# A gated attention block with experts: the gates' copy moves behind the attention's, the last two groups are closed side by side, and GpSimd takes one addition from VectorE

## The chip, the cores and the metric

One core of one Trainium2 chip. TensorE (PE) does the matrix products, VectorE (DVE), ScalarE (ACT) and GpSimd (POOL) work on 128 partitions each, SyncE starts transfers. Each engine runs its own instructions in order; they wait for each other by semaphores. The time is the device time of one execution in microseconds (us), and a change is compared by the median of several runs.

## The reference

```python
x = x + tanh(g_xattn) * xattn(layernorm(x), ctx, ctx)            # 16 heads, 32 sequences of 128
x = x + tanh(g_ffn) * ffn(layernorm(x), ...)
# ffn: rotated causal attention, then
x1 = layer_norm(x + attn_out, ln1_w, ln1_b)
gates = softmax(x1 @ gate_w.T + gate_b)                            # 8 experts, the best two are kept
moe_out = sum(expert_outputs of the best two * their gates)
return layer_norm(x1 + moe_out, ln2_w, ln2_b)
```

x is 32 x 128 x 128 in float32. The change touches only what comes behind the second attention: its output projection, the first norm, the gates, the eight experts and the second norm.

## The kernel before

The 32 sequences are worked on in 16 groups of two. The first 333 us hold both attentions, in a schedule by slots. Behind them comes `z_steps`, a loop over steps s = 3 to 21, written once for each engine as a `body(s, c)`: the order of the instructions on an engine is that in which its body calls them, and nothing else sets it. In step s the group s is projected (`transpose_att`, `project`) and gets its first norm; group s - 1 gets its normalised rows transposed (`transpose_n`), its logits and the first four experts; group s - 2 gets its gates and experts 4 to 7; group s - 3 is summed and gets the second norm; groups s - 4 and s - 5 are scaled and stored. `in_z(c, k)` says that the group s - k exists; LAST is 15. Steps 3 to 15 are whole ones; the rest only finish.

The experts: DVE multiplies the first four by their gates and adds them up (`experts`, eight instructions on `z_acc`). ACT multiplies the last four (`gate_experts`, into `z_gated`), DVE adds them in pairs (`gated_pairs`, 128x512) and then the pairs (`gated_sum`, 128x256, into `z_gated_sum`), PE adds the result to the experts' biases in `u_bank[1]`, and DVE adds the two halves (`experts_add`, into `z_x_moe`). The very last group has no pairs: PE adds its four products itself (`last_gated_sum`).

Each norm: DVE takes statistics, moments (`z_mv`) and the negative mean (`z_minus_mean`); POOL's `factor1` and `factor2` make of them the factor and the offset, three small instructions each (`z_ve`, `z_rstd`, `z_offset`, L796, L798, L1396 and L1405); ACT applies them (`normalise1` into `z_n`, `normalise2` into `z_y`). POOL also applies the norms' weights (`x1`: `z_nw` and `z_x`; `final`: `z_yw` and `z_o`).

One bank holds both the transposed attention and the transposed rows: `transpose_n` waits until ACT has copied the attention out (`copy_att`, L1021). The logits (L912) wait for ACT's copy of the transposed rows (`copy_x1`, L1028) and, since they share a bank with the transposed gates, for the copy of the gates of the group before (`copy_gates`, L1059).

## Time and profile before

| | |
|---|---|
| median of 3 runs | 440.88 us (440.47 to 441.33) |
| the profiled execution | 440.74 us, of which its span is 438.9 us |
| PE busy | 386.6 us (88% of the span) |
| DVE busy | 369.8 us (84%) |
| POOL busy | 322.9 us (74%) |
| ACT busy | 284.2 us (65%) |
| granted TensorE clock | 0.995 over the span |

The shares are means over stages that are limited by different things. Only the last quarter of the span is touched by the change, and it is read by itself: the timeline of each engine there gives the start and the length of every instruction, and in brackets the idle time before it with what ended it.

### The profile page before, as it was taken

Reading aid. Unit: us, or ns where it says so; the run is one execution under the profiler, and the core shown is the slowest. Engines: PE = TensorE matmul, PEld = TensorE weight load, DVE = VectorE, ACT = ScalarE, POOL = GpSimd, SP = SyncE. Lnnn points to the kernel's source line nnn. Section 1 sums busy time; section 2 is a strip of 40 time slices with the busy share of each in tenths; the row PEclk is TensorE's granted clock in tenths of the full one; section 3 lists DMA queues with packets and bytes.
Section 4 is the critical chain, followed back from the end, with each engine's and each line's share of the span. In section 5 each row is a group of like instructions: output and inputs, shape, how many; then the busy total and the mean of one; then the engine's idle time right before and its main releaser. Section 6 shows DMA issues by size and latency. Waiting matters only on the chain.

```text
span 438.9 us, 17690 instructions
## 1 busy us (share of the span) xinstructions
PE 386.6 (88%) x6538; PEld 231.7 (53%) x6538; DVE 369.8 (84%) x1219; ACT 284.2 (65%) x728; POOL 322.9 (74%) x712
## 2 busy tenths in 40 slices
PE   0368888888888899999999999999999999999994
PEld 0134544444444556666666666666665555555541
DVE  6587999999997877888877877878858999999987
ACT  1126777767776666666666666666665687787782
POOL 4456767767779988888888888874322688888885
PEclk9999999999999999999999999999999999999997
DMA  6756686665553333343334444333000000000001
GB/s 164 194 155 159 160 208 176 163 172 148 132 158 101 98 100 101 103 110 101 102 102 120 117 114 116 102 105 96 12 4 2 1 24 15 24 26 13 25 24 50
DMA packets 88037, 42.76 MB, mean 97 GB/s; under 512 B 16000, under 2 KB 87824, under 8 KB 87952
## 3 DMA queue, kind: packets, MB, share of 16 engines
q1 hardware_dynamic: 80864, 39.59, 33.9%
q10 hardware_dynamic: 7088, 2.04, 2.0%
q8 instruction: 53, 0.87, 0.9%
q14 instruction: 32, 0.26, 0.2%
HBM read 5.69 MB, written 2.10 MB: 18 GB/s over the span
## 4 chain that ended last, share of the span: by engine, by line
PE 48%; DVE 6%; issue 2%; ACT 2%; POOL 1%; POOLq 0%; DVEq 0%
PE u_bank L499 9%; PE s_bank L926 6%; PE st_bank L926 6%; PE s_bank L421 5%; PE s_bank L434 4%; DVE r L697 2%; PE u_bank L945 2%; PE t_bank L413 2%; PE u_bank L912 2%; PE t_bank L407 2%; PE m_bank L889 2%; PE u_bank L514 1%; PE u_bank L950 1%; PE t_bank L900 1%; ACT part L577 1%
## 5 line engine op out<-in xcount | busy, mean ns | idle before, releaser
L716 DVE TENSOR_REDUCE nm<-s_bank 128x4 f32<-128x512 f32 x256 | 171.5, 682 | 36.2 <-PE s_bank L434 33.9
L599 ACT ACTIVATE pt<-st_bank 128x512 f32<-128x512 f32 x250 | 147.4, 602 | 73.7 <-PE st_bank L434 51.2
L434 PE MATMUL s_bank<-qk 64*64 64x128 bf16 (+1 forms) x1584 | 103.6, 220 | 12.2 <-DVE nm L716 6.9
L499 PE MATMUL u_bank<-pt,vaug 128*32 128x128 f32 x2048 | 108.3, 286 | 1.7
L434 PE MATMUL st_bank<-qk 64*64 64x128 bf16 (+1 forms) x1540 | 98.2, 218 | 0.0
L434 PEld LDWEIGHTS s_bank<-qk 64*64 64x64 bf16 (+1 forms) x1584 | 73.9, 104 | 36.2 <-issue 18.9
L434 PEld LDWEIGHTS st_bank<-qk 64*64 64x64 bf16 (+1 forms) x1540 | 69.2, 103 | 0.0
L499 PEld LDWEIGHTS u_bank<-pt,vaug 128*32 128x32 f32 x2048 | 41.2, 108 | 27.6 <-issue 5.2
L421 PE MATMUL s_bank<-mqk,idb 64*64 64x256 bf16 x256 | 38.3, 292 | 0.5 <-ACT pt L599 0.4
L327 POOL TENSOR_TENSOR part<-r,part 128x512 bf16<-128x512 f32 x32 | 37.1, 1159 | 1.4
L421 PE MATMUL st_bank<-mkq,idb 64*64 64x256 bf16 x244 | 35.7, 293 | 0.0
L338 POOL TENSOR_SCALAR mst<-nm 128x16 bf16<-128x16 f32 x64 | 13.2, 207 | 27.7 <-DVE nm L716 27.7
L606 ACT ACTIVATE mts<-m_bank 128x128 bf16<-128x128 bf16 x63 | 17.5, 278 | 24.8 <-PE m_bank L509 24.8
L514 PE MATMUL u_bank<-idf,us 128*128 128x128 f32 x128 | 28.0, 301 | 5.2 <-ACT us L615 4.9
L796 POOL TENSOR_SCALAR z_ve<-z_mv 128x2 f32<-128x2 f32 x32 | 13.0, 405 | 26.5 <-DVE z_minus_mean L1162 22.6
L1068 ACT ACTIVATE z_gated<-st_bank,z_gates 128x128 f32<-128x128 f32 x120 | 31.5, 343 | 0.0
L926 PE MATMUL s_bank<-ewt,z_x_t 128*128 128x512 f32 x64 | 31.4, 613 | 0.0
L926 PE MATMUL st_bank<-ewt,z_x_t 128*128 128x512 f32 x64 | 30.2, 594 | 0.0
L322 POOL TENSOR_SCALAR part<-r 128x512 bf16<-128x512 f32 x32 | 19.9, 620 | 10.8 <-DVE r L692 6.3
L421 PEld LDWEIGHTS s_bank<-mqk,idb 64*64 64x64 bf16 x256 | 14.4, 103 | 24.3 <-issue 14.3
L1231 DVE SCALAR_TENSOR_TENSOR z_acc<-s_bank,z_gates,z_acc 128x128 f32<-128x128 f32 x96 | 26.1, 341 | 0.0
L280 POOL TENSOR_TENSOR rstd<-ve,mhalf 128x2 f32<-128x2 f32 x32 | 22.8, 713 | 2.7
(138 smaller groups left out, 828.2 us busy)
## 6 DMA issues: line engine op xcount, KB each, us to landing
qk<-part SPq DMA_DIRECT2D x221, 128.0 KB, 2.8
x_all<-x SPq DMA_DIRECT2D x16, 128.0 KB, 2.6
qk<-qrow SPq DMA_DIRECT2D x32, 64.0 KB, 2.2
c_all<-ctx_in SPq DMA_DIRECT2D x14, 128.0 KB, 2.6
out<-z_o SPq DMA_DIRECT2D x14, 128.0 KB, 1.8
qk<-mts ACTq DMA_DIRECT2D x34, 32.0 KB, 2.6
qk<-mts SPq DMA_DIRECT2D x30, 32.0 KB, 2.0
ewt<-exp_t SPq DMA_DIRECT2D x1, 512.0 KB
```

The source lines that it names most:

```text
L280: pool.tensor_tensor(rstd[u % 2][:, :], ve[u % 2][:, :], mhalf[:, :], ALU.pow).then_inc(rstd_s, 1)
L322: pool.tensor_scalar(part[u % 2][:, 1:2 * PARTS:PARTS, :], r32[:, :].rearrange("c (o t) -> c o t", o=2), 1.0, 0.0, ALU.mult, ALU.add).then ...
L327: pool.tensor_tensor(part[u % 2][:, 2:2 * PARTS:PARTS, :], r32[:, :].rearrange("c (o t) -> c o t", o=2), part[u % 2][:, 1:2 * PARTS:PARTS, ...
L421: pe.matmul(to, idb[rows, rows], mask[rows, rows].unsqueeze(1).broadcast_to([64, HEADS, 64]), start=True, stop=False, skip_group_check=True)
L434: ins = pe.matmul(to[outs, :], fixed[:, outs], moving, start=not masked, stop=True, skip_group_check=masked)
L499: ins = pe.matmul(u_bank[b][32 * j:32 * j + 32, r * P:(r + 1) * P], v, pt[m % 4][:, j, :], start=half == 0, stop=half == 1, skip_group_che ...
L514: ins = pe.transpose(u_bank[q % 2][:, W + r * P:W + (r + 1) * P], us[q % 2][:, r * P:(r + 1) * P], idf[:, :])
L599: act.activation(pt[m % 4][:, :, :].rearrange("k j q -> k (j q)"), transposed_bank(m)[:, :], ACT.Exp).then_inc(ex, 1)
L716: dve.tensor_reduce(nm[q % 2][:, first:first + HEADS], s_bank[n % 2][:, :].rearrange("q (j k) -> q j k", j=HEADS), AX_X, ALU.max, negate=T ...
L926: ins = pe.matmul(e_bank[b][k][:, :], zx1t[i][:, b * P:(b + 1) * P], ewt[:, k * 512:(k + 1) * 512], start=True, stop=True)
L1068: ins = act.activation(zyg[:, b, e, :], e_bank[b][1][:, e * P:(e + 1) * P], ACT.Copy, scale=zg[i][:, b, HALF + e:HALF + e + 1])
L1231: dve.scalar_tensor_tensor(out=zacc[i][e % 2][:, b, :], in0=e_bank[b][0][:, e * P:(e + 1) * P], scalar=zg[i][:, b, e:e + 1], in1=zacc[i][( ...
```

## The change

1. ACT copies the gates (`copy_gates`) right behind `copy_att` and ahead of `copy_x1`, except for the last group.
2. `gated_sum`, the addition of the two pairs, goes from DVE to POOL, between `factor1` and `factor2`, for the groups 0 to 13. Group 14's stays on DVE.
3. DVE takes the first norm's moments ahead of the second norm's statistics, and the pairs come ahead of the second norm's `experts_minus_mean`. `factor1` starts when the moments are there; only its third instruction waits for the negative mean. `factor2` likewise.
4. The last two groups: their sums, statistics and moments are taken side by side in the last step, `factor2(14)` moves there, and PE transposes the gates of group 14 ahead of the rows of group 15. On ACT `normalise2` of group 13 goes behind the last experts.

```diff
--- before.py
+++ after.py
@@ -842,8 +842,9 @@
         def rstd_steps(g):
             return 2 * g if g <= 2 else 3 * g - 2
 
-        def all_steps(g):
-            return (g + 1) * ALL - (1 if g == LAST else 0)
+        def moments_done(g):
+            both = (LAST - 1) * ALL + G + G * G
+            return (g + 1) * ALL - 1 if g < LAST - 1 else both + (g - LAST + 2) * G
 
         def in_z(c, lag):
             return 0 <= c - lag < GROUPS
@@ -966,10 +967,11 @@
                 if in_z(c, 0):
                     transpose_att(s, c)
                 if s - 1 == LAST:
+                    gates_t(s - 2, c - 2)
                     transpose_n(s - 1, c - 1)
                 if in_z(c, 3) and s - 3 < LAST:
                     sum_of_biases(s - 3, c - 3)
-                if in_z(c, 2):
+                if in_z(c, 2) and s - 1 != LAST:
                     gates_t(s - 2, c - 2)
                 if in_z(c, 1) and s - 1 < LAST:
                     transpose_n(s - 1, c - 1)
@@ -1083,14 +1085,10 @@
             def body(s, c):
                 if in_z(c, 0):
                     copy_att(s, c)
+                if in_z(c, 2) and s - 2 < LAST:
+                    copy_gates(s - 2, c - 2)
                 if in_z(c, 1):
                     copy_x1(s - 1, c - 1)
-                if in_z(c, 4) and s - 2 == LAST:
-                    normalise2(s - 4, c - 4)
-                if s - 2 == LAST:
-                    gate_last_experts(s - 2, c - 2)
-                if in_z(c, 2):
-                    copy_gates(s - 2, c - 2)
                 if in_z(c, 2) and s - 2 < LAST:
                     gate_experts(s - 2, c - 2, 0)
                     if s - 1 == LAST:
@@ -1098,7 +1096,10 @@
                     gate_experts(s - 2, c - 2, 1)
                     if s - 1 < LAST:
                         gates_exp(s - 1, c - 1)
-                if in_z(c, 4) and s - 2 < LAST:
+                if s - 2 == LAST:
+                    gate_last_experts(s - 2, c - 2)
+                    copy_gates(s - 2, c - 2)
+                if in_z(c, 4) and s - 4 < LAST - 1:
                     normalise2(s - 4, c - 4)
                 if in_z(c, 0):
                     normalise1(s, c)
@@ -1192,7 +1193,7 @@
                 add_gate_bias(g, gc)
                 logit_maxima(g, gc)
 
-            def gating(g, gc, second_level=None):
+            def gating(g, gc):
 
 
                 i = gc % 2
@@ -1208,8 +1209,6 @@
                 dve.wait_ge(z_gate, k + 6)
                 for b in range(G):
                     dve.match_replace(zq[:, b, :], z8[:, b, :], zp[:, b, :], 0.0).then_inc(z_gate, 1)
-                if second_level is not None:
-                    gated_sum(*second_level)
                 dve.wait_ge(z_gate, k + 9)
                 dve.tensor_tensor(zt[:, :, :], zp[:, :, :], zq[:, :, :], ALU.subtract).then_inc(z_gate, 1)
                 dve.wait_ge(z_gate, k + 10)
@@ -1260,20 +1259,19 @@
             def experts_stats(g, gc):
                 k = g * ALL
                 y = zsum[g % 2]
-                dve.wait_ge(z_all, k + 1)
+                dve.wait_ge(z_all, k + 1 if g < LAST - 1 else (LAST - 1) * ALL + G)
                 for b in range(G):
                     dve.bn_stats(zst2[g % 2][:, b, :], y[:, b, :]).then_inc(z_all, 1)
 
             def experts_moments(g, gc):
                 k = g * ALL
-                dve.wait_ge(z_all, k + 1 + G)
+                dve.wait_ge(z_all, k + 1 + G if g < LAST - 1 else (LAST - 1) * ALL + G + G * G)
                 for b in range(G):
                     dve.bn_aggr(zmv2[g % 2][:, b, :], zst2[g % 2][:, b, :]).then_inc(z_all, 1)
 
             def experts_minus_mean(g, gc):
-                if g < LAST:
-                    dve.wait_ge(z_all, (g + 1) * ALL - 1)
-                    dve.tensor_scalar(zmn2[g % 2][:, :], zmv2[g % 2][:, :, 0], -1.0, 0.0, ALU.mult, ALU.add).then_inc(z_all, 1)
+                dve.wait_ge(z_all, (g + 1) * ALL - 1)
+                dve.tensor_scalar(zmn2[g % 2][:, :], zmv2[g % 2][:, :, 0], -1.0, 0.0, ALU.mult, ALU.add).then_inc(z_all, 1)
 
 
             def all_experts(g, gc):
@@ -1284,7 +1282,7 @@
 
             def weigh(g):
                 i = g % 2
-                dve.wait_ge(z_all, all_steps(g))
+                dve.wait_ge(z_all, moments_done(g))
                 for b in range(G):
                     dve.scalar_tensor_tensor(out=zyc[i][:, b, :], in0=zsum[i][:, b, :], scalar=zmv2[i][:, b, 0:1],
                                              in1=l2w[:, :], op0=ALU.subtract, op1=ALU.mult).then_inc(z_yw, 1)
@@ -1302,7 +1300,9 @@
                 if in_z(c, 2) and s - 2 < LAST:
                     if in_z(c, 3):
                         gated_pairs(s - 3, c - 3)
-                    gating(s - 2, c - 2, (s - 3, c - 3) if in_z(c, 3) else None)
+                    if in_z(c, 4):
+                        experts_minus_mean(s - 4, c - 4)
+                    gating(s - 2, c - 2)
                 if s - 2 == LAST:
                     gating(s - 2, c - 2)
                     gated_pairs(s - 3, c - 3)
@@ -1312,24 +1312,25 @@
                 if in_z(c, 0):
                     attention_add(s, c)
                     experts_add(s - 3, c - 3)
+                    attention_stats(s, c)
                     add_gate_bias(s - 1, c - 1)
-                    attention_stats(s, c)
+                    attention_moments(s, c)
                     logit_maxima(s - 1, c - 1)
                     experts_stats(s - 3, c - 3)
-                    attention_moments(s, c)
+                    attention_minus_mean(s, c)
                     experts_moments(s - 3, c - 3)
-                    attention_minus_mean(s, c)
-                    experts_minus_mean(s - 3, c - 3)
                 else:
                     if s - 1 == LAST:
                         shift_logits(s - 1, c - 1)
-                    if in_z(c, 3):
+                    if s - 3 == LAST - 2:
                         all_experts(s - 3, c - 3)
-                    if s - 3 == LAST - 1:
+                    if s - 3 == LAST:
+                        for step in (experts_add, experts_stats, experts_moments):
+                            step(LAST - 1, c - 4)
+                            step(LAST, c - 3)
                         weigh(LAST - 1)
-                    if s - 3 == LAST:
+                        weigh(LAST)
                         close(LAST - 1)
-                        weigh(LAST)
                         close(LAST)
 
             def early(n):
@@ -1372,6 +1373,12 @@
                 pool.tensor_tensor(zx1[i][:, :, :], zw[:, :, :], l1b[:, :].unsqueeze(1).broadcast_to([P, G, P]),
                                    ALU.add).then_inc(z_x1, 1)
 
+            def gated_sum(g, gc):
+                pool.wait_ge(z_yp, g + 1)
+                if gc >= 1:
+                    pool.wait_ge(z_yb, g)
+                pool.tensor_tensor(zyq[:, :, :], zyp[:, :, 0, :], zyp[:, :, 1, :], ALU.add).then_inc(z_yq, 1)
+
             def final(g, gc):
                 i = gc % 2
                 pool.wait_ge(z_y2s, (g + 1) * G)
@@ -1387,27 +1394,30 @@
 
             def factor1(g, gc):
                 i = gc % 2
-                pool.wait_ge(z_h, (g + 1) * H1)
+                pool.wait_ge(z_h, (g + 1) * H1 - 1)
                 if gc >= 2:
                     pool.wait_ge(z_n, (g - 1) * G)
                 rstd_of(pool, zmv[i][:, :, 1], zve[i][:, :], zrs[i][:, :], z_rs, rstd_steps(g))
                 if g >= 2:
                     pool.wait_ge(z_rs, rstd_steps(g) + 2)
+                    pool.wait_ge(z_h, (g + 1) * H1)
                     pool.tensor_tensor(znb[i][:, :], zmn[i][:, :], zrs[i][:, :], ALU.mult).then_inc(z_rs, 1)
 
             def factor2(g, gc):
                 i = g % 2
-                pool.wait_ge(z_all, all_steps(g))
+                pool.wait_ge(z_all, moments_done(g))
                 k = g * 3 if g < LAST else (LAST - 1) * 3 + 2
                 rstd_of(pool, zmv2[i][:, :, 1], zve2[i][:, :], zrs2[i][:, :], z_rs2, k)
                 if g < LAST - 1:
                     pool.wait_ge(z_rs2, k + 2)
+                    pool.wait_ge(z_all, (g + 1) * ALL)
                     pool.tensor_tensor(znb2[i][:, :], zmn2[i][:, :], zrs2[i][:, :], ALU.mult).then_inc(z_rs2, 1)
 
             def body(s, c):
                 if in_z(c, 1):
                     x1(s - 1, c - 1)
                 if s - 3 == LAST:
+                    factor2(s - 4, c - 4)
                     factor2(s - 3, c - 3)
                 if in_z(c, 5) and s - 5 < LAST - 2:
                     final(s - 5, c - 5)
@@ -1415,7 +1425,8 @@
                     final(s - 4, c - 4)
                 if in_z(c, 0):
                     factor1(s, c)
-                if in_z(c, 3) and s - 3 < LAST:
+                    gated_sum(s - 2, c - 2)
+                if in_z(c, 3) and s - 3 < LAST - 1:
                     factor2(s - 3, c - 3)
 
             def early(n):
@@ -1441,6 +1452,7 @@
 
             def steps():
                 factor1(2, 2)
+                gated_sum(0, 0)
                 z_steps(body)
 
             return early, steps
```

DVE in a whole step of before (`z_h` is the sum behind the first norm, `z_x_moe` that behind the second; `z_mv_1` and `z_minus_mean_1` belong to the second norm, as does any name there with a number):

```order
L1144 TENSOR_TENSOR z_h<-m_bank,xn_all 128x256
L1257 TENSOR_TENSOR z_x_moe<-u_bank,z_acc 128x256
L1183 TENSOR_TENSOR z_logit<-u_bank,gbb 128x16
L1151 BN_STATS z_stats<-z_h 128x6 x2
L1189 TENSOR_REDUCE z_max<-z_logit 128x2
L1265 BN_STATS z_stats_1<-z_x_moe 128x6 x2
L1157 BN_AGGR z_mv<-z_stats 128x2 x2
L1271 BN_AGGR z_mv_1<-z_stats_1 128x2 x2
L1162 TENSOR_SCALAR z_minus_mean<-z_mv 128x2
L1276 TENSOR_SCALAR z_minus_mean_1<-z_mv_1 128x2
L1240 TENSOR_TENSOR z_gated_pairs<-z_gated 128x512
```

and the same place now:

```order
L1145 TENSOR_TENSOR z_h<-m_bank,xn_all 128x256
L1256 TENSOR_TENSOR z_x_moe<-u_bank,z_acc 128x256
L1152 BN_STATS z_stats<-z_h 128x6 x2
L1184 TENSOR_TENSOR z_logit<-u_bank,gbb 128x16
L1158 BN_AGGR z_mv<-z_stats 128x2 x2
L1190 TENSOR_REDUCE z_max<-z_logit 128x2
L1264 BN_STATS z_stats_1<-z_x_moe 128x6 x2
L1163 TENSOR_SCALAR z_minus_mean<-z_mv 128x2
L1270 BN_AGGR z_mv_1<-z_stats_1 128x2 x2
L1239 TENSOR_TENSOR z_gated_pairs<-z_gated 128x512
L1274 TENSOR_SCALAR z_minus_mean_1<-z_mv_1 128x2
L1203 MAX z_sorted<-z_exps 128x8 x2
```

The first norm's moments (`z_mv`) now come ahead of the maxima and of the second statistics, and the pairs ahead of the second negative mean; the addition into `z_gated_sum`, which stood further down ahead of `z_top`, is gone.

POOL in a whole step of before:

```order
L1367 TENSOR_TENSOR z_nw<-z_n,l1w 128x256
L1372 TENSOR_TENSOR z_x<-z_nw,l1b 128x256
L1380 TENSOR_TENSOR z_yw<-z_y,l2w 128x256
L1386 TENSOR_TENSOR z_o<-z_yw,x_all 128x256
L796 TENSOR_SCALAR z_ve<-z_mv 128x2
L798 TENSOR_TENSOR z_rstd<-z_ve,mhalf 128x2
L1396 TENSOR_TENSOR z_offset<-z_minus_mean,z_rstd 128x2
L796 TENSOR_SCALAR z_ve_1<-z_mv_1 128x2
L798 TENSOR_TENSOR z_rstd_1<-z_ve_1,mhalf 128x2
L1405 TENSOR_TENSOR z_offset_1<-z_minus_mean_1,z_rstd_1 128x2
```

and now:

```order
L1368 TENSOR_TENSOR z_nw<-z_n,l1w 128x256
L1373 TENSOR_TENSOR z_x<-z_nw,l1b 128x256
L1387 TENSOR_TENSOR z_yw<-z_y,l2w 128x256
L1393 TENSOR_TENSOR z_o<-z_yw,x_all 128x256
L796 TENSOR_SCALAR z_ve<-z_mv 128x2
L798 TENSOR_TENSOR z_rstd<-z_ve,mhalf 128x2
L1404 TENSOR_TENSOR z_offset<-z_minus_mean,z_rstd 128x2
L1380 TENSOR_TENSOR z_gated_sum<-z_gated_pairs 128x256
L796 TENSOR_SCALAR z_ve_1<-z_mv_1 128x2
L798 TENSOR_TENSOR z_rstd_1<-z_ve_1,mhalf 128x2
L1414 TENSOR_TENSOR z_offset_1<-z_minus_mean_1,z_rstd_1 128x2
```

The addition stands between the two norms' factors.

DVE at the end of before, from the last product of group 15 on:

```order
L1231 SCALAR_TENSOR_TENSOR z_acc<-s_bank,z_gates,z_acc 128x128 x6
L1257 TENSOR_TENSOR z_x_moe<-u_bank,z_acc 128x256
L1265 BN_STATS z_stats_0<-z_x_moe 128x6 x2
L1271 BN_AGGR z_mv_0<-z_stats_0 128x2 x2
L1276 TENSOR_SCALAR z_minus_mean_0<-z_mv_0 128x2
L1289 SCALAR_TENSOR_TENSOR z_yc<-z_x_moe,z_mv_0,l2w 128x128 x2
L1257 TENSOR_TENSOR z_x_moe<-t_bank,z_acc 128x256
L1265 BN_STATS z_stats_1<-z_x_moe 128x6 x2
L1271 BN_AGGR z_mv_1<-z_stats_1 128x2 x2
L1298 SCALAR_TENSOR_TENSOR z_o<-z_yc,z_rstd_0,x_all 128x128 x2
L1289 SCALAR_TENSOR_TENSOR z_yc<-z_x_moe,z_mv_1,l2w 128x128 x2
L1298 SCALAR_TENSOR_TENSOR z_o<-z_yc,z_rstd_1,x_all 128x128 x2
```

and now:

```order
L1256 TENSOR_TENSOR z_x_moe<-u_bank,z_acc 128x256
L1256 TENSOR_TENSOR z_x_moe<-t_bank,z_acc 128x256
L1264 BN_STATS z_stats_0<-z_x_moe 128x6 x2
L1264 BN_STATS z_stats_1<-z_x_moe 128x6 x2
L1270 BN_AGGR z_mv_0<-z_stats_0 128x2 x2
L1270 BN_AGGR z_mv_1<-z_stats_1 128x2 x2
L1287 SCALAR_TENSOR_TENSOR z_yc<-z_x_moe,z_mv_0,l2w 128x128 x2
L1287 SCALAR_TENSOR_TENSOR z_yc<-z_x_moe,z_mv_1,l2w 128x128 x2
L1296 SCALAR_TENSOR_TENSOR z_o<-z_yc,z_rstd_0,x_all 128x128 x2
L1296 SCALAR_TENSOR_TENSOR z_o<-z_yc,z_rstd_1,x_all 128x128 x2
```

Both sums come first and both closing pairs last, and the negative mean of group 14 is gone.

## Rows read from the trace of the kernel before

**Rows 1.** Timeline: PE: start us, length us, engine, line, operation, count.

```profile
416.26 0.28 PE L935 MATMUL u_bank<-idf,z_gates 128*16 128x128 f32 x1
416.65 0.41 PE L900 MATMUL t_bank<-idf,z_n 128*128 128x128 f32 x2
...
417.95 0.58 PE L912 MATMUL u_bank<-gwt,z_x_t 128*128 128x8 f32 x4
...
423.87 0.28 PE L935 MATMUL u_bank<-idf,z_gates 128*16 128x128 f32 x1
423.98 0.60 PE L950 MATMUL u_bank<-z_gated_sum,idf 128*128 128x256 f32 x2
```

**Rows 2.** Timeline: DVE, the period from 411.38 us, same columns.

```profile
411.38 0.42 DVE L1144 TENSOR_TENSOR z_h<-m_bank,xn_all 128x256 f32<-128x256 f32 x1 [0.25 <-PE m_bank L889]
...
412.53 0.15 DVE L1189 TENSOR_REDUCE z_max<-z_logit 128x2 f32<-128x16 f32 x1
...
412.99 0.23 DVE L1157 BATCH_NORM_AGGREGATE z_mv<-z_stats 128x2 f32<-128x6 f32 x2
...
413.47 0.69 DVE L1240 TENSOR_TENSOR z_gated_pairs<-z_gated 128x512 f32<-128x512 f32 x1
...
414.76 0.42 DVE L1247 TENSOR_TENSOR z_gated_sum<-z_gated_pairs 128x256 f32<-128x256 f32 x1
415.09 0.17 DVE L1214 TENSOR_TENSOR z_top<-z_exps,z_others 128x16 f32<-128x16 f32 x1
...
417.97 0.42 DVE L1144 TENSOR_TENSOR z_h<-m_bank,xn_all 128x256 f32<-128x256 f32 x1 [0.25 <-PE m_bank L889]
```

**Rows 3.** Timeline: POOL, the same period.

```profile
413.51 0.70 POOL L796 TENSOR_SCALAR z_ve<-z_mv 128x2 f32<-128x2 f32 x1 [0.47 <-DVE z_minus_mean L1162]
414.30 0.70 POOL L798 TENSOR_TENSOR z_rstd<-z_ve,mhalf 128x2 f32<-128x2 f32 x1
415.08 0.25 POOL L1396 TENSOR_TENSOR z_offset<-z_minus_mean,z_rstd 128x2 f32<-128x2 f32 x1
415.41 0.19 POOL L796 TENSOR_SCALAR z_ve<-z_mv 128x2 f32<-128x2 f32 x1
...
416.45 0.20 POOL L1405 TENSOR_TENSOR z_offset<-z_minus_mean,z_rstd 128x2 f32<-128x2 f32 x1
416.61 0.73 POOL L1367 TENSOR_TENSOR z_nw<-z_n,l1w 128x256 f32<-128x256 f32 x1
417.41 0.73 POOL L1372 TENSOR_TENSOR z_x<-z_nw,l1b 128x256 f32<-128x256 f32 x1
418.09 0.73 POOL L1380 TENSOR_TENSOR z_yw<-z_y,l2w 128x256 f32<-128x256 f32 x1
```

**Rows 4.** Timeline: ACT, the same period.

```profile
415.36 0.88 ACT L1045 ACTIVATE z_n<-z_h,z_offset,z_rstd 128x128 f32<-128x128 f32 x2 [0.98 <-POOL z_offset L1396]
...
417.09 0.56 ACT L1028 ACTIVATE z_x_t<-t_bank,l1bc,l1wc 128x256 f32<-128x256 f32 x1 [0.59 <-PE t_bank L900]
417.56 0.25 ACT L1059 ACTIVATE z_gates_t<-u_bank 16x128 f32<-16x128 f32 x1
```

**Rows 5.** Timeline: POOL in the attention, a large instruction and a small one.

```profile
157.17 1.16 POOL L327 TENSOR_TENSOR part<-r,part 128x512 bf16<-128x512 f32 x1
158.42 0.20 POOL L277 TENSOR_SCALAR ve<-mv 128x2 f32<-128x2 f32 x1
```

**Rows 6.** Timeline: POOL and DVE at the same time in step 17.

```profile
428.68 0.72 POOL L1380 TENSOR_TENSOR z_yw<-z_y,l2w 128x256 f32<-128x256 f32 x1
428.69 0.98 DVE L1247 TENSOR_TENSOR z_gated_sum<-z_gated_pairs 128x256 f32<-128x256 f32 x1
```

**Rows 7.** Timeline: the end: timelines of DVE and, last row, POOL.

```profile
429.60 0.60 DVE L1231 SCALAR_TENSOR_TENSOR z_acc<-s_bank,z_gates,z_x 128x128 f32<-128x128 f32 x2
...
433.65 0.41 DVE L1257 TENSOR_TENSOR z_x_moe<-t_bank,z_acc 128x256 f32<-128x256 f32 x1
...
434.96 0.20 POOL L796 TENSOR_SCALAR z_ve<-z_mv 128x2 f32<-128x2 f32 x1 [0.65 <-DVE z_mv L1271]
```

## The prediction

> **What bounds the kernel now.** The chain that ended last comes first: from 333 us on it lies on PE almost alone, which reads as if PE were the limit. The timeline of each engine over one period behind 400 us corrects that. From one `z_h` to the next are 417.97 - 411.38 = 6.59 us [rows 2], and each of the steps 3 to 15 repeats it. In it PE stands still twice. Between the transposed gates and the transposed rows lie 0.39 us, where the same instruction gives way after 0.11 in the next step, in another place [rows 1]: 0.28 us of waiting, for ACT, which copies the attention only after its normalisation. And the logits at 417.95 come after the copy of the gates, which ends at 417.56 + 0.25 = 417.81, while the rows themselves were copied at 417.09 + 0.56 = 417.65 [rows 4]: 0.16 us, at most 0.18. PE's own work is 6.59 - 0.28 - 0.18 = 6.13 us a step. So the period is a loop: `z_h`, statistics, moments and negative mean on DVE, three instructions on POOL, normalisation on ACT (idle 0.98 us for POOL's offset [rows 4]), copy, transposes, projection, `z_h`.
>
> Inside the loop one row is odd. POOL's first `z_ve` takes 0.70 us, the second, on equal shapes, 0.19 [rows 3]. It starts at 413.51, just behind the start of the pairs on DVE, 413.47 to 414.16 [rows 2]: it is held up by 0.51 us and ends 0.05 behind them. The reverse is in [rows 6]: a DVE addition that alone takes 0.42 [rows 2] takes 0.98 because a POOL addition began 0.01 us before it; it goes on about 0.14 ahead of POOL's end (428.68 + 0.72 - 0.14 = 429.26, and 429.26 + 0.42 = 429.68). So these two kinds shut each other out, and the loser's own time starts 0.14 ahead of the winner's end.
>
> **Part 1, gates copied earlier.** Nothing is added. The logits come 0.16 to 0.18 earlier on PE; the copy itself (0.16 us of ACT's queue) goes ahead of `z_x_t`, where ACT is idle for 0.59 [rows 4]. Taken alone it cuts the loop by nothing, as the logits aren't on it; it lowers what PE needs.
>
> **Part 2 and 3, the loop.** DVE loses the addition, 415.09 - 414.76 = 0.33 us, but the wait that it covered (`z_others` to `z_top`) shows: about 0.11 comes back. The new order costs about 0.06 in waits on the statistics. DVE needs about 6.1 us a step. `z_ve` may start after the moments. Before, it started 413.51 - 411.38 = 2.13 behind `z_h`. The maxima and the second statistics, 412.99 - 412.53 = 0.46 [rows 2], no longer stand ahead of the moments, nor do the second moments and the negative mean (0.20); the wait for the statistics takes 0.03 to 0.05 of it back: 1.50. From the unhindered start of `z_ve` to the start of `z_n`: 0.28 + (415.36 - 414.30 = 1.06) = 1.34 [rows 3, 4]. From there to `z_h`: 417.97 - 415.36 = 2.61 [rows 2, 4]. The loop shrinks to 1.50 + 1.34 + 2.61 = 5.45 us and stops being the limit.
>
> **What is late next** is POOL. Its queue, start to start, from [rows 3]: `z_ve` 0.27; `z_rstd` 415.08 - 414.30 = 0.78; `z_offset` 416.61 - 416.45 = 0.16; the new addition 0.81; `z_ve` 0.27 and `z_rstd` 0.77 (together 416.45 - 415.41 = 1.04); `z_offset` 0.16; `z_nw` 417.41 - 416.61 = 0.80; `z_x` 0.68; `z_yw` 0.81 as `z_nw`, since the next one needs its result; `z_o` 0.81. The sum is 6.32 us. No row shows the addition on POOL. I take 0.73 us, the time of the four other additions and products of this shape, and 0.08 until a small `z_ve` follows, as in 415.08 + 0.25 = 415.33 to 415.41 [rows 3] and 157.17 + 1.16 = 158.33 to 158.42 behind a large one [rows 5]. The lower bound lets the next instruction start 0.04 ahead of the end, as `z_x` to `z_yw` does: 0.69 in place of 0.81 at two places, sum 6.08. The upper bound is the longest hold-up seen, 0.51, on top. A gain is excluded: the work is added.
>
> **The pairs meet POOL.** POOL's queue is 6.32 long and the loop 5.45, so `z_ve` comes to its turn 0.87 us after its moments are there, 1.50 + 0.87 = 2.37 behind `z_h`, and `z_o` stands ahead of it from 1.56 to 2.29. On DVE the pairs come to their turn 413.47 - 411.38 = 2.09 behind `z_h`, less the negative mean that went behind them, plus waits: about 2.06 [rows 2]. That is inside `z_o`. DVE waits until 2.29 - 0.14 = 2.15, runs the 0.69 us to 2.84, and `z_ve` goes on at 2.84 - 0.14 = 2.70 in place of 2.37. That is 0.33 us for POOL, the limit: 6.65 us a step. The hold-up lengthens the queue and the loop alike, so it does not move out of its own way.
>
> The Trainium skill (SBUF — State Buffer, "SBUF: two separate sides") says the port pair that DVE and GpSimd share is an exclusive lock, taken by a DVE operation with two SBUF inputs against a GpSimd one that reads SBUF, and that the loser is blocked until about 115 ns behind DVE's end. The trace agrees on the lock [rows 3, 6] and not on the length: `z_ve` would have ended at 414.16 + 0.12 + 0.19 = 414.47 and ended at 414.21. By the page's figure a step would take 6.90 us by estimate and the kernel 443 us.
>
> **The sum.** Steps 3 and 4 have no `z_yw` and `z_o` on POOL and no collision: PE's 6.13, taken as 6.16 with the loop's joints, saves 2 x 0.43 = 0.86. While POOL falls behind, the two steps after them meet the pairs at other instructions; laid forward by hand they take about 6.47 and save 2 x 0.12 = 0.24. The eight periods to step 15 cost 8 x 0.06 = 0.5 more. So the last `z_h` comes 0.6 us earlier.
>
> **The end (part 4).** Before, from the start of the last products at 429.60 [rows 7] to the end of the last `z_o` are 7.00 us, with the last sum at 433.65, 4.05 behind. Now that sum waits only for PE's last additions, which ACT feeds 0.8 us earlier: it comes 3.14 behind. But both groups' statistics and POOL's factors now follow one another. Sum 0.33, statistics 0.39 twice, moments 0.13 and 0.22 and 0.09: POOL starts 4.6 behind, held up by 0.17 by DVE's products; `z_ve` 0.27 and `z_rstd` 0.78 for group 14, again 0.17, then the same for 15; last, 0.61 for the closing pair: 7.6. In before the last `z_ve` started 434.96 - 429.60 = 5.36 behind [rows 7], now 5.9. That is 0.6 lost. Ahead of it, the earlier gates of group 14 and ACT's shorter queue save 0.2, and the 0.56 that DVE lost in [rows 6] is a tie of 0.01 us that may fall either way: 0 to 0.7. The end costs between -0.3 and +0.4. Total: -0.9 to -0.2; I take -0.45. On the profiled execution's 440.74 us (the median of the runs is 0.14 above it) that is 440.3 us. A measurement can tell about 0.2% here, 0.9 us: 440.0 to 441.76 is no change.
>
> **Rivals.** (A) The forecast, POOL bound with the pairs in its way, 440.3 us: chance 0.50, of which 0.1 falls below 440.0. (B) POOL bound but the pairs find a gap: 6.32 a step. For it: in [rows 6] the order was decided by 0.01 us. Against: the arithmetic puts the pairs 0.2 us inside `z_o`. Ten steps x 0.27 + 0.86 = 3.6 saved: 437.1 us, chance 0.22. (C) Slower: the hold-up is dearer than 0.33. The pairs come so late in `z_o`, or `z_ve` loses to them so early, that the whole 0.51 of [rows 3] is paid, or the offset is held up too (0.05 of its 0.25 us, [rows 3]). It decides from 6.67 us a step on, where the gain of the first steps is gone. At 6.80 it is 10 x 0.21 - 0.86 = +1.2: 442.0 us; with both, 6.32 + 0.51 + 0.05 = 6.88, it is 442.8. Chance 0.20. By the figure of the Trainium skill's page above it would end in this rival as well. (D) The addition finds room: POOL's queue at its lower bound of 6.08 lies below PE's 6.13, and 12 steps x 0.43 go: 435.6 us, chance 0.08. That the copy of the gates doesn't free the logits, because the transposed gates come late, changes nothing while POOL is the limit.
>
> **The numbers.** Faster 0.1 + 0.22 + 0.08 = 0.40; slower 0.18, most of C; within 0.2% 0.42. The range leaves out D and the upper part of C: 436.8 to 442.2; A alone has 439.8 to 441.2.
>
> **What would show it.** ACT's gates' copy ahead of `z_x_t` and no gap over 0.05 ahead of the logits: part 1. POOL without idle from step 6 on, `z_o`, `z_ve` and the pairs within 0.3 us, `z_ve` about 0.5 long and the pairs over 0.8: A. The same with `z_ve` 0.19: B. Periods of 6.16 in steps 3 and 4, then 6.65. At the end `z_ve` of both groups 1.2 us apart. Wrong is the forecast if POOL still idles ahead of `z_ve`.

## The result, and the profile after

The changed kernel takes 443.19 us (median of 6 runs, 442.65 to 444.04), the kernel before 440.91 us beside it (440.47 to 441.33). The ratio is 1.0053 with a 95% interval of 1.0040 to 1.0066: slower by 2.3 us, more than a measurement can miss, and outside the range of the prediction. The profiled execution has a time of 443.27 us and a span of 441.4 us, 2.5 more than before.

| | before | after |
|---|---|---|
| `z_h` of step 3 to step 4, us | 6.59 | 6.08 |
| steady period, us | 6.59 | 6.86 |
| last `z_h` starts, us | 417.97 | 419.21 |
| from there to the end of the last `z_o` on DVE, us | 18.62 | 19.80 |

The table shows both halves of the loss. The first `z_h` of the steps already stands 0.2 us late; steps 2 to 4 give back 0.05 + 0.51 + 0.52; then come 6.48, 6.63 and eight periods of 6.86, 0.27 longer than before: the last `z_h` is 1.24 us late. The end is 1.18 us longer.

The busy times of the page (first row before, second after): POOL took over DVE's additions and more.

```profile
PE 386.6 (88%) x6538; PEld 231.7 (53%) x6538; DVE 369.8 (84%) x1219; ACT 284.2 (65%) x728; POOL 322.9 (74%) x712
```

```profile
PE 384.0 (87%) x6538; PEld 231.9 (53%) x6538; DVE 370.2 (84%) x1204; ACT 285.6 (65%) x728; POOL 330.6 (75%) x726
```

DVE runs 15 instructions fewer and is busy 0.4 us longer: something there now takes longer than its work. One steady period, timeline of DVE after (start us, length us, engine, line, operation); it answers to [rows 2]:

```profile
398.63 0.42 DVE L1145 TENSOR_TENSOR z_h<-m_bank,xn_all 128x256 f32<-128x256 f32 x1 [0.34 <-PE m_bank L890]
...
399.81 0.25 DVE L1158 BATCH_NORM_AGGREGATE z_mv<-z_stats 128x2 f32<-128x6 f32 x2
...
400.03 0.48 DVE L1264 BATCH_NORM_STATS2 z_stats<-z_x_moe 128x6 f32<-128x128 f32 x2
400.42 0.58 DVE L1163 TENSOR_SCALAR z_minus_mean<-z_mv 128x2 f32<-128x2 f32 x1
400.92 0.23 DVE L1270 BATCH_NORM_AGGREGATE z_mv<-z_stats 128x2 f32<-128x6 f32 x2
401.08 0.65 DVE L1239 TENSOR_TENSOR z_gated_pairs<-z_gated 128x512 f32<-128x512 f32 x1
401.65 0.15 DVE L1274 TENSOR_SCALAR z_minus_mean<-z_mv 128x2 f32<-128x2 f32 x1
```

And POOL in the same period, where [rows 3] had five large instructions and a wait:

```profile
400.26 0.72 POOL L1393 TENSOR_TENSOR z_o<-z_yw,x_all 128x256 f32<-128x256 f32 x1
401.06 0.71 POOL L796 TENSOR_SCALAR z_ve<-z_mv 128x2 f32<-128x2 f32 x1
401.86 0.70 POOL L798 TENSOR_TENSOR z_rstd<-z_ve,mhalf 128x2 f32<-128x2 f32 x1
402.64 0.20 POOL L1404 TENSOR_TENSOR z_offset<-z_minus_mean,z_rstd 128x2 f32<-128x2 f32 x1
402.80 0.73 POOL L1380 TENSOR_TENSOR z_gated_sum<-z_gated_pairs 128x256 f32<-128x256 f32 x1
403.61 0.19 POOL L796 TENSOR_SCALAR z_ve<-z_mv 128x2 f32<-128x2 f32 x1
```

Read them side by side. POOL has no idle time any more: it is the limit. Its `z_o` starts at 400.26, `z_minus_mean` on DVE at 400.42. The same operation on the same shape takes 0.15 us at 401.65 and 0.58 here; it ends at 401.00, which is `z_o`'s end less 0.14 (400.84) plus its own 0.15. So `z_o` holds it up by 0.43. Behind it everything on DVE is later, and the pairs start at 401.08, 0.02 us after `z_ve` on POOL (401.06). It is `z_ve` that loses all the same, though its record starts first: its 0.19 become 0.71, and it ends 0.04 behind the pairs. This chain of two hold-ups repeats in each steady period; its price for POOL, the limit, is 0.52 us: 6.33 us of queue + 0.52 = 6.85.

### The profile page after: what moved, and what is told of

It is laid out like the page before. It is cut to its first block, busy times and chain, and to the rows that moved or that the text cites. A ratio compares the mean times of both kernels' runs of the same rounds, so it can differ in the third digit from the quotient of the medians.

```text
span 441.4 us, 17717 instructions
## 1 busy us (share of the span) xinstructions
PE 384.0 (87%) x6538; PEld 231.9 (53%) x6538; DVE 370.2 (84%) x1204; ACT 285.6 (65%) x728; POOL 330.6 (75%) x726
## 4 chain that ended last, share of the span: by engine, by line
PE 33%; DVE 14%; POOL 4%; issue 3%; ACT 3%; POOLq 0%; DVEq 0%; ACTq 0%
PE u_bank L499 9%; PE s_bank L421 5%; PE s_bank L434 4%; DVE r L697 2%; PE t_bank L413 2%; DVE z_acc L1230 2%; PE t_bank L407 2%; POOL z_ve L796 2%; POOL z_rstd L798 2%; DVE z_stats L1264 1%; PE u_bank L514 1%; DVE z_x_moe L1256 1%; ACT part L577 1%; DVE z_stats L1152 1%; PE m_bank L890 1%
## 5 line engine op out<-in xcount | busy, mean ns | idle before, releaser
L1070 ACT ACTIVATE z_gated<-st_bank,z_gates 128x128 f32<-128x128 f32 x120 | 32.5, 383 | 0.0
L796 POOL TENSOR_SCALAR z_ve<-z_mv 128x2 f32<-128x2 f32 x32 | 11.7, 367 | 19.9 <-DVE z_mv L1158 16.5
L798 POOL TENSOR_TENSOR z_rstd<-z_ve,mhalf 128x2 f32<-128x2 f32 x32 | 22.9, 716 | 2.7
```

The lines of the kernel that those rows point to most:

```text
L796: pool.tensor_scalar(v_eps, v_in, 1.0, EPS, ALU.mult, ALU.add).then_inc(semaphore, 1)
L798: pool.tensor_tensor(r_out, v_eps, mhalf[:, :], ALU.pow).then_inc(semaphore, 1)
L1070: ins = act.activation(zyg[:, b, e, :], e_bank[b][1][:, e * P:(e + 1) * P], ACT.Copy, scale=zg[i][:, b, HALF + e:HALF + e + 1])
```

## The experiments

The table puts all kernels beside each other; "after the last `z_h`" is the time to the end of the last `z_o`, and both it and the period are of the profiled execution alone. The kernels before that ran beside them had medians of 440.72 us (the first four), 440.92 (the next four) and 440.91 (the last).

| kernel | median us | ratio to before, 95% | period | after the last `z_h` |
|---|---|---|---|---|
| after | 443.19 | 1.0040 to 1.0066 | 6.86 | 19.80 |
| before, gates copied early | 440.53 | 0.9979 to 1.0006 | 6.59 | 18.36 |
| after, sum back on DVE | 437.06 | 0.9901 to 0.9933 | 6.29 | 18.49 |
| after, means by a reduction | 441.08 | 0.9998 to 1.0024 | 6.65 | 20.59 |
| after, end as before | 442.11 | 1.0027 to 1.0063 | 6.85 | 18.94 |
| after, sum on DVE, end as before | 436.69 | 0.9884 to 0.9914 | 6.29 | 17.85 |
| the same, means by a reduction | 436.49 | 0.9879 to 0.9908 | 6.29 | 17.86 |
| after, POOL's factor and sum first | 441.20 | 0.9998 to 1.0027 | 6.62 | 18.81 |
| before, only the sum on POOL | 443.06 | 1.0027 to 1.0061 | 6.79 | 19.26 |
| before, only DVE's new order | 436.22 | 0.9878 to 0.9911 | 6.29 | 17.31 |

**The gates' copy alone.** The kernel before with part 1, and PE transposing the gates first in the last step:

```diff
                 if in_z(c, 0):
                     copy_att(s, c)
+                if in_z(c, 2) and s - 2 < LAST:
+                    copy_gates(s - 2, c - 2)
                 if in_z(c, 1):
                     copy_x1(s - 1, c - 1)
...
-                if in_z(c, 2):
+                if s - 2 == LAST:
                     copy_gates(s - 2, c - 2)
```

> The kernel before with part 1 alone: ACT copies the gates right behind the attention, and PE transposes the gates of group 14 ahead of the rows of group 15. Theory (the period is the loop over POOL's factor, the logits are not on it): the period stays 6.59 us, the logits come 0.16 us earlier and wait for nothing; 440.9 us, between 440.5 and 441.4. Rival (the logits are on the path): 12 x 0.16 = 1.9 us less, 439.0 us.

Measured 440.53 us, period 6.59: no change, as forecast. ACT copies the gates ahead of `z_x_t`, the logits start 0.20 us ahead of `z_h` (404.41 and 404.61) where they started 0.02 ahead, and the period does not move: the logits are not on the loop.

**The sum back on DVE.** The changed kernel without part 2:

```diff
                     dve.match_replace(zq[:, b, :], z8[:, b, :], zp[:, b, :], 0.0).then_inc(z_gate, 1)
+                if second_level is not None:
+                    gated_sum(*second_level)
...
                     factor1(s, c)
-                    gated_sum(s - 2, c - 2)
```

> The changed kernel with the second level of the gated sum back on DVE, all else kept. Theory (POOL's queue, 6.33 us with the addition and 6.86 with what DVE does to it, is the limit): without the addition POOL's queue is 5.5 us, it idles ahead of z_ve, z_ve takes 0.19 and the negative mean 0.15; the period falls to about 6.3 us and the kernel to 438.5 us, between 437.5 and 439.5. Rival (the moments ahead of the second statistics, or the side by side end, made it slower): 442 us or more.

Measured 437.06 us: 6.1 us below the changed kernel, and 0.8% below the kernel before. POOL in a period:

```profile
395.85 0.73 POOL L1395 TENSOR_TENSOR z_o<-z_yw,x_all 128x256 f32<-128x256 f32 x1
397.30 0.19 POOL L796 TENSOR_SCALAR z_ve<-z_mv 128x2 f32<-128x2 f32 x1 [0.72 <-DVE z_mv L1158]
```

POOL waits 0.72 us for the moments again, `z_o` is long over when DVE takes the mean, and `z_ve` takes its 0.19. Now DVE has no idle time and its queue of 6.29 us is the period (one period, from 382.92 us on, is 6.59: DVE starts its pairs late with no wait that the profile names; the other runs with 6.29 have such a period in about the same place, and its cause is open). The period is the expected one; the total is 1.4 us better than expected and just outside the stated 437.5 to 439.5. The whole loss comes with the sum's move, and hardly any of it is work: of the 6.86 - 6.29 = 0.57 us a period 0.52 are the hold-up, and POOL's queue alone (6.33) is 0.04 longer than this period. Another 1.3 us lie behind the last `z_h`.

**The two means as a reduction.** In the changed kernel the negative mean of both norms is taken by an instruction of another kind, on the same values:

```diff
-dve.tensor_scalar(zmn[i][:, :], zmv[i][:, :, 0], -1.0, 0.0, ALU.mult, ALU.add).then_inc(z_h, 1)
+dve.tensor_reduce(zmn[i][:, :], zmv[i][:, :, 0:1], AX_X, ALU.max, negate=True).then_inc(z_h, 1)
```

> The changed kernel, but both negative means are taken by a TENSOR_REDUCE over one element with its sign turned (same values) in place of a TENSOR_SCALAR. Theory (the TENSOR_SCALAR, though it has one input, is held up by POOL's z_o for 0.43 us and so brings the pairs exactly onto z_ve, which then waits 0.52): the reduction takes 0.15 us, the pairs come 0.4 us earlier and wait inside z_o, z_ve takes about 0.5 in place of 0.72, the period falls from 6.86 to about 6.65 us and the kernel to 441.1 us. Rival (any small DVE instruction is held up there, or the moments themselves come late): the period stays 6.86 and the time 443.2 us.

Measured 441.08 us. This is the run that isolates the step that failed. DVE, then POOL:

```profile
398.87 0.13 DVE L1163 TENSOR_REDUCE z_minus_mean<-z_mv 128x2 f32<-128x2 f32 x1
398.98 0.25 DVE L1270 BATCH_NORM_AGGREGATE z_mv<-z_stats 128x2 f32<-128x6 f32 x2
399.15 0.83 DVE L1239 TENSOR_TENSOR z_gated_pairs<-z_gated 128x512 f32<-128x512 f32 x1
```

```profile
398.70 0.73 POOL L1393 TENSOR_TENSOR z_o<-z_yw,x_all 128x256 f32<-128x256 f32 x1
399.51 0.51 POOL L796 TENSOR_SCALAR z_ve<-z_mv 128x2 f32<-128x2 f32 x1
```

The reduction starts inside `z_o` (398.70 to 399.43) and takes 0.13 us: it is not held up. The pairs come 2.08 us behind `z_h` (397.07), still inside `z_o`, wait, run to 399.98, and hold `z_ve` for 0.51 - 0.19 = 0.32 in place of 0.52. That is the prediction's picture, number by number: pairs at 2.06, hold-up 0.33, period 6.65; and the two periods behind step 5 are 6.48 each, where the prediction had 6.47 twice. Five of its ten executions lie between 440.79 and 440.95, half a microsecond above the forecast's 440.3, with an end that is longer than forecast; four lie at 441.9 to 442.5, and the last section shows what one of them has more.

**The end as before**, in the changed kernel: the pair before last is summed and weighed first, the last pair behind it.

```diff
-                    if s - 3 == LAST - 2:
+                    if s - 3 < LAST - 1:
                         all_experts(s - 3, c - 3)
-                    if s - 3 == LAST:
+                    if s - 3 in (LAST - 1, LAST):
                         for step in (experts_add, experts_stats, experts_moments):
...
-                    factor2(s - 4, c - 4)
                     factor2(s - 3, c - 3)
```

> The changed kernel with the end of DVE and POOL as before: group 14 is summed, and its factors taken, in its own step, and group 15's behind it. Theory (the side by side end costs about 0.4 us, since both groups' factors follow one another on POOL behind the last moments): 442.8 us. Rival (the end is long because POOL arrives late, whatever the order): 443.2 us or more, and if side by side is a gain, up to 443.9 us.

Measured 442.11 us, and 18.94 us behind the last `z_h` against 19.80: the order of the end costs 0.86 us, twice what was expected, and the median lies below the expected 442.8. The end of the changed kernel on DVE, answering to [rows 7], and its POOL:

```profile
431.10 0.59 DVE L1230 SCALAR_TENSOR_TENSOR z_acc<-s_bank,z_gates,z_x 128x128 f32<-128x128 f32 x2
...
434.32 0.42 DVE L1256 TENSOR_TENSOR z_x_moe<-t_bank,z_acc 128x256 f32<-128x256 f32 x1 [0.74 <-PE t_bank L962]
434.78 0.87 DVE L1264 BATCH_NORM_STATS2 z_stats<-z_x_moe 128x6 f32<-128x128 f32 x4
435.69 0.38 DVE L1270 BATCH_NORM_AGGREGATE z_mv<-z_stats 128x2 f32<-128x6 f32 x4
...
438.40 0.61 DVE L1296 SCALAR_TENSOR_TENSOR z_o<-z_yc,z_rstd,x_all 128x128 f32<-128x128 f32 x2 [0.60 <-POOL z_rstd L798]
```

```profile
436.02 0.35 POOL L796 TENSOR_SCALAR z_ve<-z_mv 128x2 f32<-128x2 f32 x1 [1.11 <-DVE z_mv L1270]
436.46 0.70 POOL L798 TENSOR_TENSOR z_rstd<-z_ve,mhalf 128x2 f32<-128x2 f32 x1
437.24 0.35 POOL L796 TENSOR_SCALAR z_ve<-z_mv 128x2 f32<-128x2 f32 x1
437.68 0.69 POOL L798 TENSOR_TENSOR z_rstd<-z_ve,mhalf 128x2 f32<-128x2 f32 x1
```

DVE idles 0.74 us for PE with the earlier group's statistics undone; then both groups' statistics and both factors on POOL stand one behind the other, and DVE idles 0.60 more for the last of them.

**Sum on DVE and the old end** (the second and the fourth run's edits together):

> The changed kernel with the second level of the gated sum back on VectorE inside the gating, and with the end of VectorE and GpSimd ordered as in the kernel before (the pair before last weighed first, the last pair behind it). The run with only the sum put back took 437.06 us with a period of 6.29 us and 18.49 us from the last attention sum to the end; the run with only the old end was 0.85 us shorter behind its last attention sum than the changed kernel (18.94 against 19.79). Theory (the loop's time is set by the meetings of GpSimd's long additions with small VectorE operations, the end costs on its own by its order): period again 6.29, last attention sum at about 414.7, end 17.7 to 18.2 behind it, 436.3 us (435.9 to 436.9). Rival (in the run with the sum put back the order of the end is hidden, because VectorE arrives there earlier by the same amount as everything else and waits for the same products): 437.06 again, within 0.3.

Measured 436.69 us, 17.85 us behind the last `z_h` against 18.49: the order of the end counts here too. Between the medians it is 0.4 us, hardly more than a few runs can tell.

**The same with reductions** (the third run's edit on top):

> The same kernel as the one with the sum on VectorE and the old end, and both negative means taken as a tensor_reduce (max, negated) over one element instead of a tensor_scalar. There no GpSimd addition is in flight when the means are taken (in the run with the sum on VectorE the tensor_scalar took 0.15 us), so theory: nothing to win, 0.01 us a step at most, same period 6.29 and same time within 0.2 us. Rival (a tensor_scalar also takes something from GpSimd, or the reduction shifts the order of arrivals so that another operation is held up): period off by more than 0.05, time off by 0.5 us or more.

Measured 436.49 us, period 6.29. As expected, the kind of instruction is worth nothing where no addition of POOL is in flight: the gain of the third run was the hold-up, not a quicker instruction.

**POOL's factor and sum first.** The same instructions in another order:

```diff
-                if in_z(c, 5) and s - 5 < LAST - 2:
-                    final(s - 5, c - 5)
...
                 if in_z(c, 0):
                     factor1(s, c)
                     gated_sum(s - 2, c - 2)
+                if in_z(c, 5) and s - 5 < LAST - 2:
+                    final(s - 5, c - 5)
```

> The changed kernel with GpSimd's queue in another order: the factor of the attention norm and the second level of the sum ahead of the final weigh-and-add of the pair five steps back (z_yw, z_o), instead of behind them; all instructions are the same, so GpSimd's queue is still 6.33 us of work. Theory (the lost time is two hold-ups that hang on where z_o stands: z_o holds up VectorE's negative mean, which pushes the pairs onto GpSimd's z_ve): with z_o behind, neither mean nor z_ve is held up (0.15 and 0.19 us), at most a gate operation meets one of GpSimd's long additions (0.4 us on VectorE, off the path of GpSimd), so the period is 6.33 to 6.5, last attention sum near 415.8 to 416.5, total 438.5 to 439.5 us, faster than before by 1.2 to 2.2 us. Rival (the cost of the addition is GpSimd's port contention in general, whatever the order): period 6.8 to 6.9, 443 us.

Measured 441.20 us, period 6.62, last `z_h` at 417.66: theory and rival both missed their numbers. The price of the sum does hang on POOL's order, so it is not the same whatever the order; but the period is above the expected 6.33 to 6.5, and the time above the expected 438.5 to 439.5. Neither the mean (0.15) nor `z_ve` (0.19) is held up any more. In their place:

```profile
399.87 0.66 DVE L1239 TENSOR_TENSOR z_gated_pairs<-z_gated 128x512 f32<-128x512 f32 x1
...
401.32 0.73 DVE L1213 TENSOR_TENSOR z_top<-z_exps,z_others 128x16 f32<-128x16 f32 x1
```

```profile
399.59 0.71 POOL L798 TENSOR_TENSOR z_rstd<-z_ve,mhalf 128x2 f32<-128x2 f32 x1
400.38 0.21 POOL L1404 TENSOR_TENSOR z_offset<-z_minus_mean,z_rstd 128x2 f32<-128x2 f32 x1
400.61 0.73 POOL L1380 TENSOR_TENSOR z_gated_sum<-z_gated_pairs 128x256 f32<-128x256 f32 x1
401.29 0.72 POOL L1387 TENSOR_TENSOR z_yw<-z_y,l2w 128x256 f32<-128x256 f32 x1
```

`z_top`, 0.17 us of work, starts 0.03 us behind `z_yw` and takes 0.73. The gates and the experts come 0.56 later. DVE is never idle in this period, and its queue is 6.29 - 0.33 (the sum gone) + 0.11 (the wait that it covered, the prediction's figure) + 0.56 = 6.63. The expectation had allowed a gate operation to lose 0.4 us, off GpSimd's path; it lost 0.56, and DVE, never idle here, sets the period. Moving the large additions moves the hold-up to another small operation; it does not go.

**Only the sum on POOL**, in the kernel before:

```diff
-                    gating(s - 2, c - 2, (s - 3, c - 3) if in_z(c, 3) else None)
+                    gating(s - 2, c - 2)
...
                     factor1(s, c)
+                    gated_sum(s - 2, c - 2)
```

> The kernel before with only one part of the change: the second level of the gated sum on GpSimd between its two factors; VectorE keeps its old order (gate bias and maxima ahead of the moments, the two negative means behind), the gates are copied late, and the end is the old one. Theory (GpSimd's queue is then the bound, and its z_ve waits for moments that come late): mean and z_ve are both held up, period 6.8 to 6.9, last attention sum at about 420.5, total 443 to 444 us, slower than the changed kernel by 0 to 1 us. Rival (the early moments of the change are what makes the meetings of z_o with the mean, and the old order has none): period 6.3 to 6.5, 438 to 440 us.

Measured 443.06 us, at the lower end of the theory's range, and 0.1 below the changed kernel, not above it. Period 6.79, just under the expected 6.8, the mean held up by 0.32 and `z_ve` by 0.43:

```profile
401.07 0.47 DVE L1162 TENSOR_SCALAR z_minus_mean<-z_mv 128x2 f32<-128x2 f32 x1
```

```profile
400.79 0.72 POOL L1392 TENSOR_TENSOR z_o<-z_yw,x_all 128x256 f32<-128x256 f32 x1
401.63 0.62 POOL L796 TENSOR_SCALAR z_ve<-z_mv 128x2 f32<-128x2 f32 x1
```

The nearest relative is the changed kernel with the old end (442.11 us, period 6.85), which has DVE's new order and the early gates besides. In the steady steps the new order is then worth nothing: what it gives is taken back by the meetings. Only the first steps gain (6.08 where this kernel has 6.52). The end of this run is not quite comparable: its profile has PE at a granted clock of 0.52 from 427.00 to 430.00, and from the last products to the end it takes 7.43 us where before has 7.00; all four executions have the same mean clock, 0.992. The sum's price depends on what stands beside it: 2.1 us here, in DVE's old order, and 6.1 us in the new one.

**Only DVE's new order**, in the kernel before. The moments go ahead, the second negative mean goes behind the pairs, the sum stays. The end keeps its old order, without the negative mean of group 14:

```diff
                     attention_add(s, c)
                     experts_add(s - 3, c - 3)
+                    attention_stats(s, c)
                     add_gate_bias(s - 1, c - 1)
-                    attention_stats(s, c)
+                    attention_moments(s, c)
                     logit_maxima(s - 1, c - 1)
                     experts_stats(s - 3, c - 3)
-                    attention_moments(s, c)
                     attention_minus_mean(s, c)
...
-                pool.wait_ge(z_h, (g + 1) * H1)
+                pool.wait_ge(z_h, (g + 1) * H1 - 1)
```

> The kernel before with only VectorE's reordering: attention moments ahead of the logit maxima, the expert moments last, the experts' negative mean moved behind the pairs, and GpSimd's factors released by the moments instead of by the means. The sum stays on VectorE, the gates are copied late, the end is the old one; it is the run of the sum on VectorE with the old end (436.69 us, period 6.29) without the early copy of the gates. Theory (the reordering is what wins: VectorE's pairs no longer meet z_ve, and the early copy of the gates is not on the loop here either): period 6.29, 436.5 to 437.0 us. Rival (with the loop at 6.29 us and TensorE's own need at 6.13 us, the earlier gates copy now carries part of it): period 6.35 to 6.45, 437.5 to 439 us.

Measured 436.22 us, period 6.29, ratio 0.9895 (0.9878 to 0.9911): the fastest of all. DVE has no idle time in the period. One part of the change holds the whole gain:

```profile
395.76 0.41 DVE L1144 TENSOR_TENSOR z_h<-m_bank,xn_all 128x256 f32<-128x256 f32 x1
...
397.83 0.66 DVE L1240 TENSOR_TENSOR z_gated_pairs<-z_gated 128x512 f32<-128x512 f32 x1
398.40 0.16 DVE L1275 TENSOR_SCALAR z_minus_mean<-z_mv 128x2 f32<-128x2 f32 x1
```

```profile
397.27 0.19 POOL L796 TENSOR_SCALAR z_ve<-z_mv 128x2 f32<-128x2 f32 x1 [0.72 <-DVE z_mv L1157]
397.55 0.71 POOL L798 TENSOR_TENSOR z_rstd<-z_ve,mhalf 128x2 f32<-128x2 f32 x1
```

`z_ve` is over (397.46) before the pairs start (397.83).

Stacked by medians from before: DVE's order -4.7 us; the gates' early copy with its order in the last steps +0.5 (436.22 to 436.69, with overlapping intervals; it is not shown to cost); the side-by-side end +0.4; the sum on POOL +6.1: together +2.3.

## Why the prediction was wrong

**What held.** The limit before was a loop and not PE; without it the loop falls below the queues (6.29 in four runs). Part 1 alone gives nothing. The addition costs 0.73 us and 0.08 on POOL, the queue is 6.33 (6.32), POOL has no idle time. `z_o` stands 1.63 to 2.35 behind `z_h` (1.56 to 2.29). The steps 3 and 4 gained 0.51 and 0.52 (0.43), those behind them came to 6.48 and 6.63 (6.47 twice). The lock's release 0.14 us ahead of the winner's end gives the measured end of every hold-up here to within 0.03.

**The step that failed** is the one that brings the pairs to their turn on DVE about 2.06 behind `z_h`. It carried `z_minus_mean` at its 0.15 us through `z_o`, because I had read the lock as one of DVE operations with two SBUF inputs. The mean has one. It is held up all the same, by 0.43: the pairs come at 401.08 - 398.63 = 2.45, not in `z_o` but just behind `z_ve`, which pays 0.52 and not 0.33. 6.86 instead of 6.65, over eight periods 1.7 us. The forecast worked with the rows at hand, which show a large operation against a large one and `z_ve` against the pairs; no row of before shows the mean beside a POOL addition, and that unknown should have been bounded from 0 to 0.5 us, as the text did for the addition. The run with reductions confirms the rest of the step: with the mean free, the pairs come at 2.08 and the period is 6.65.

The Trainium skill has the half of the rule that I left out. In the section that I cited (SBUF — State Buffer, "SBUF: two separate sides"), the lock is also taken by an operation in a mode that uses both of DVE's read ports; and (VectorE: DVE Perf Modes, "The perf-mode tier table") `tensor_scalar` on fp32 in SBUF has such a mode, `tensor_reduce` has only the plain one. The traces fit both: inside POOL's `z_o` the one takes 0.58 us and the other 0.13, down to two elements a partition. They don't show which mode an instruction runs in, so that this is the reason is not shown; that the kind of instruction decides is.

**The rival.** This was (C): the whole 0.51 is paid, 6.86 a step where it said 6.80 to 6.88, 443.27 us where it said 442.0 to 442.8. Its condition, pairs so late that `z_ve` pays in full, was given a small chance; the mean made it the rule. The estimate of 6.90 us a step and 443 us that the prediction worked out from the Trainium skill's figure comes near by luck: it had the pairs inside `z_o` and a release behind the winner's end, and neither is what the trace shows.

**The end** was mis-sized: 7.91 us (439.01 - 431.10) from the last products, not 7.6, where before has 7.00. The sum came at 3.22 (3.14), `z_ve` at 4.92 behind (4.6). Part of that is adding up: the prediction's own terms give 4.69 and then 7.74. The rest is that the terms for the sum and the four statistics had back-to-back spacing, where each now waits for the one ahead of it (0.46 for 0.33, and 0.91 for 0.78). The tie of [rows 6] was lost again (`z_gated_sum` 0.98 us). Forecast -0.3 to +0.4, measured +0.9 for the seven-us stretch; 0.26 more lie between the last `z_h` and those products, where the experts' mean, held up by `z_o` on POOL from 427.71 on, takes 0.41 us and not 0.15:

```profile
428.06 0.41 DVE L1274 TENSOR_SCALAR z_minus_mean<-z_mv 128x2 f32<-128x2 f32 x1
```

**Sum.** Forecast -0.6 for the last `z_h`, measured +1.24: 1.7 of it the hold-up, 0.2 a later start, less 0.1 for better first steps. Forecast +0.15 for the end, measured +1.18. The chance that I gave to slower, 0.18, rested on (C) alone being an accident.

## What to carry to other kernels

Before work goes from DVE to GpSimd, write down for one period which large GpSimd operations will be in flight and every DVE operation that starts inside them, small ones with one SBUF input too; each may pay up to the rest of the GpSimd operation, and what it pushes back can then hold up GpSimd in turn. Where no row shows the pair in question, bound it from nothing to the whole. Test the parts of a change one by one: here one reordering was worth 4.7 us, and the offload that came with it cost 6.1, though in the kernel before it alone cost 2.1. Let the last groups follow each other rather than march side by side when one wait stands ahead of both.

## What the runs showed of the hardware

**Small instructions count in full.** A `tensor_scalar` over two elements a partition lost 0.43 us to an addition on GpSimd, a `tensor_reduce` on the same values nothing. Nor did the statistics lose: the two of `z_h` start at 399.30, inside GpSimd's `z_x` (398.77, 0.73 us), and take 0.47 us, as long as two take in the kernel before at 432.11 with GpSimd idle (0.48).

**Not every `tensor_scalar` loses.** The attention of the kernel before has one with two per-partition scalars that starts inside GpSimd's own, and takes the 0.34 us that it also takes at 161.30, where GpSimd's had ended. Whether DVE's instruction or GpSimd's makes the difference no run here tells:

```profile
201.64 0.84 POOL L284 TENSOR_SCALAR xn_all<-x_all,mv,rstd 128x128 f32<-128x128 f32 x1
```

```profile
202.00 0.34 DVE L684 TENSOR_SCALAR xn_all<-x_all,mv,rstd 128x128 f32<-128x128 f32 x1
```

**The length of a GpSimd instruction is not what blocks.** `z_rstd` takes 0.70 us on two elements, as long as an addition over 256. In the run with the factor first, DVE's pairs start at 399.87, inside it (399.59 to 400.30), and take their 0.66 us, unhindered. Yet it is held up itself when the pairs start first, here in the changed kernel by 0.45 us (DVE, then POOL):

```profile
353.28 0.66 DVE L1239 TENSOR_TENSOR z_gated_pairs<-z_gated 128x512 f32<-128x512 f32 x1
```

```profile
353.36 1.15 POOL L798 TENSOR_TENSOR z_rstd<-z_ve,mhalf 128x2 f32<-128x2 f32 x1
```

**The clock falls in some executions.** In the profiled one of the kernel with reductions, the granted clock by windows (length, PE busy, PEclk, DMA share, GB/s):

```profile
421.00:422.00 1.00, 0.28 (x2) 1.00 0.00 0
422.00:424.00 2.00, 2.00 (x11) 1.00 0.03 8
424.00:427.00 3.00, 3.00 (x5) 0.51 0.01 3
427.00:428.00 1.00, 1.00 (x3) 0.77 0.40 121
```

From 424.0 on PE has 1.2 instead of 2.4 GHz for about 3.4 us. It had stood mostly still from 421 to 422 and was busy throughout from 422 to 424, and the four products take 3.62 us and not 1.96. DVE waits 1.94 us for PE at the end in place of 0.74: 20.59 us behind the last `z_h`. Four of that kernel's ten executions are 0.7 to 1.7 us above the others, with a mean granted clock of 0.990 to 0.994 against 0.994 to 0.997; in the run with POOL's factor first it is three of ten (442.5 to 443.0 us at 0.990 to 0.993, the others 440.5 to 441.8), in the one with the old end three of seven (443.2 to 443.8 at 0.993 and 0.994, the others 441.7 to 442.1 at 0.997 and 0.998). Only one of these executions was profiled, so for the others a like stretch is an inference from the mean clock. The profiled execution of the changed kernel stands still as long (PE is busy for 0.48 of the 1.50 us from 423.00 to 424.50) and keeps the full clock to 438. What decides it was not tried.
